# Scores of the second layer from 32 rows of the matrix array, issued in batches of four

## What is computed

```python
for layer in (0, 1):
    h = layernorm(x) * (1 + ca) + sa
    x = x + ga * attention(h)
    h = layernorm(x) * (1 + cb) + sb
    x = x + gb * experts(h)          # 8 experts; top 1 in layer 0, top 2 in layer 1

# attention of layer 0: causal
dots = q @ k.T * scale ; masked ; softmax ; @ v ; @ Wout.T + bout
# attention of layer 1: not causal, and followed by a second attention over two past states
output = softmax(q @ k.T * scale) @ v @ Wo + bo
rq = output @ Wrq + brq ; rk, rv = past @ Wrk + brk, past @ Wrv + brv     # 2 x 256 past tokens
rctx = mean over the two pasts of softmax(rq @ rk.T * scale) @ rv
gate = sigmoid([output, rctx] @ Wg + bg)
output = output * (1 - gate) + rctx * gate
```

## Time and profile before

| | |
|---|---|
| median of 3 runs | 1052.02 us |
| time of the profiled execution | 1054.27 us |
| span of its trace | 1052.3 us |
| PE busy | 960.2 us, 91% |
| DVE busy | 788.7 us, 75% |
| ACT busy | 591.6 us, 56% |
| POOL busy | 228.7 us, 22% |
| scores of layer 1 | from 360.71 us to about 894 us |
| experts of layer 1 and the end | from about 895 us |

### The profile page before, as it was taken

One profiled execution on the slowest core, in us unless ns is written; L12 is line 12 of the kernel. 1 busy time (PEld: TensorE's weight loads), 2 busy tenths in 40 slices (PEclk: granted clock), 3 DMA queues, 4 the chain that ended last, 5 costly groups with the idle time before them and its releaser, 6 DMA issues.

```text
span 1052.3 us, 17558 instructions
## 1 busy us (share of the span) xinstructions
PE 960.2 (91%) x5970; PEld 639.5 (61%) x5970; DVE 788.7 (75%) x2196; ACT 591.6 (56%) x1270; POOL 228.7 (22%) x360
## 2 busy tenths in 40 slices
PE   8889998888878989999999999999899887999992
PEld 7555665555668645555555555555555442999992
DVE  6888888776465698778888788978878784686673
ACT  2466565454555445767677676775567656443330
POOL 6132323263213234000000100001032112120073
PEclk8899999898989989999999999999999989999996
DMA  4334310010112111110000000000070000212132
GB/s 124 91 99 138 91 51 21 11 50 12 36 37 75 29 28 31 31 41 2 1 11 21 11 1 2 21 14 8 1 260 21 1 3 29 74 44 61 34 86 68
DMA packets 56497, 46.50 MB, mean 44 GB/s; under 512 B 6742, under 2 KB 46038, under 8 KB 56408
## 3 DMA queue, kind: packets, MB, share of 16 engines
q1 hardware_dynamic: 41960, 33.77, 11.4%
q0 software_dynamic: 3072, 6.30, 2.1%
q10 hardware_dynamic: 11376, 5.32, 1.8%
HBM read 22.55 MB, written 14.16 MB: 35 GB/s over the span
## 4 chain that ended last, share of the span: by engine, by line
PE 66%; DVE 20%; POOL 5%; issue 4%; ACT 2%; DMA 2%; DVEq 1%; SPq 0%; POOLq 0%; ACTq 0%
PE st L1346 13%; PE pv L1368 13%; PE ring L1332 12%; PE ring L1249 7%; PE ring L1469 4%; DVE ring L1653 4%; PE st L1456 3%; PE ring L1260 2%; PE ring L1299 2%; DVE M L1649 2%; PE st L1462 2%; DVE M L1656 2%; PE pv L1462 2%; POOL G L1041 1%; PE pv L1279 1%
## 5 line engine op out<-in xcount | busy, mean ns | idle before, releaser
L1123 ACT ACTIVATE Et<-st 128x512 f32<-128x512 f32 (+3 forms) x768 | 380.9, 548 | 211.9 <-PE st L1346 208.2
L1332 PE MATMUL ring<-Kbd,Qa 128*128 128x512 f32 (+3 forms) x512 | 203.3, 417 | 17.4 <-DVE M L1653 7.7
L1346 PE MATMUL st<-Qb,Kbd 128*128 128x512 f32 (+3 forms) x512 | 196.4, 399 | 4.4 <-ACT Et L1123 4.3
L1656 DVE TENSOR_REDUCE M<-ring 128x1 f32<-128x512 f32 x256 | 163.8, 683 | 38.4 <-PE ring L1332 37.0
L1649 DVE TENSOR_REDUCE M<-ring 128x2 f32<-128x512 f32 x256 | 162.9, 683 | 28.6 <-PE ring L1332 27.8
L1346 PEld LDWEIGHTS st<-Qb,Kbd 128*128 128x128 f32 x512 | 96.9, 195 | 89.6 <-ACT Et L1123 65.5
L1332 PEld LDWEIGHTS ring<-Kbd,Qa 128*128 128x128 f32 x512 | 100.6, 200 | 61.8 <-DVE M L1656 19.7
L1653 DVE CUSTOM_DVE_ANT_0 ring<-ring,maskw 128x128 f32<-128x128 f32 (+3 forms) x256 | 120.7, 510 | 20.9 <-PE ring L1332 19.5
L1368 PE MATMUL pv<-Et,Va 128*32 128x512 f32 (+3 forms) x1024 | 120.9, 533 | 0.7 <-POOL Et L984 0.7
L1332 PE MATMUL ring<-RKbd,Qa 128*128 128x512 f32 x256 | 108.2, 430 | 7.0 <-DVE M L1649 6.3
L1346 PE MATMUL st<-Qb,RKbd 128*128 128x512 f32 x256 | 105.4, 427 | 1.2 <-ACT Et L1123 1.0
(11 more groups left out here) (222 smaller groups left out, 1263.6 us busy)
## 6 DMA issues: line engine op xcount, KB each, us to landing
Kbd<-Ksb SPq DMA_DIRECT2D x116, 64.0 KB, 2.0
Yd<-Yt ACTq DMA_DIRECT2D x76, 64.0 KB, 1.5
Xs<-Xd SPq DMA_DIRECT2D x16, 256.0 KB, 3.0
L1W<-in_L1W SPq DMA_DIRECT2D x2, 2048.0 KB, 11.8
Xd<-zero SPq DMA_DIRECT2D x6, 512.0 KB, 3.5
W<-in_L0W SPq DMA_DIRECT2D x8, 258.0 KB, 3.5
W<-in_L0W SPq DMA_DIRECT2D x8, 256.0 KB, 4.2
Xd<-zero SPq DMA_DIRECT2D x4, 448.0 KB, 4.4
```

The lines of the kernel that those rows point to most:

```text
L1123: e.activation(Et[s // 2 % 4][:, j % 2, q0:512], st[s % NST][:, q0:512], ACT.Exp, scale=SCALE).then_inc(exp_done, 1)
L1332: ins = nc.tensor.matmul(bank(ph)[:, 0:n], Qa[u % 2][:, t * 128:(t + 1) * 128], kb[:, j, 0:n], start=True, stop=True)
L1346: nc.tensor.matmul(st[s % NST][:, q0:512], kb[:, j, c * 128:(c + 1) * 128], Qb[u % 2][:, q0:512], start=True, stop=True).then_inc(st_full, 1)
L1656: e.tensor_reduce(M[i][:, t, j, 0:1], bank(ph)[:, 0:n], AX.X, ALU.max).then_inc(mx_red, 1)
```

## The change

Layer 0 is left as it is. In layer 1:

- `mx` and `st` of head j multiply 32 rows instead of 128: `Qa[32j:32j+32]` by the keys on the same partitions, which are now simply the transposed keys (`KT` for self units, `RKT` for the past). ScalarE writes these straight from PSUM. The DMAs from `Ksb`, the block diagonals, their zeroing by GpSimd and the semaphores for them are gone in layer 1.
- The order of the plan is new. `mx` and `st` come in pairs every second step: heads 2 and 3 of the one beside heads 0 and 1 of the other, then the other way round. So four matmuls in a row stand on four different strips of 32 rows and write to four different banks. `pv`, `kT`, `qT`, `qbT`, `norm` and the other generators are started on the odd steps between. `FRONT`, `BACK` and others get a value for each layer.
- `ones_ahead`: one or two products of ones are put ahead of `rq`, `oTr` and `gate`, ahead of each pair of `mx` in units 0 and 1 of layer 1, and ahead of each pair of `st` in units 29 to 31. They go into the bank that the phase will overwrite.
- The end of the second attention (`epi_rec`: `oTr`, `gate`, `blend`) starts 9 or 5 steps later for the first two sequences and 3 for the third, and `token_rows` of layer 1 start 1 and 7 steps later. The wait in `mcol` to `qbT` is 3 steps instead of 4.

```diff
-KPREP, QPREP, FRONT, BACK = 2, 7, 10, 34
-AFTER_MAX, FINISH, PREP = 4, 2, -24
+KPREP, QPREP, FRONT, BACK = (2, 3), 7, (10, 12), (34, 36)
+AFTER_MAX, FINISH, PREP = (4, 3), (2, 3), (-24, -23)
...
+def ones_ahead(ph):
+
+    if ph[0] in ("rq", "oTr", "gate"):
+        return 2
+    if ph[0] == "mx" and ph[1] == 1 and ph[2] < 2 and ph[4] % 2 == 0:
+        return 2
+    return 1 if ph[0] == "st" and ph[1] == 1 and ph[2] >= 29 and ph[4] % 2 == 0 else 0
...
     def front(l, u, unit):
         for t in range(4):
...
+            else:
+                for j in (2, 3):
+                    do("mx", l, u, t, j)
+                yield from wait(2)
+                for j in (0, 1):
+                    do("mx", l, u, t, j)
+                yield from wait(2)
...
     def back(l, u, unit, starts, at):
...
+            do("st", l, u, c, 0)
+            do("st", l, u, c, 1)
+            yield
+            if c:
+                do("pv", l, u, c - 1)
+            yield
+            do("st", l, u, c, 2)
+            do("st", l, u, c, 3)
+            yield from wait(2)
+        yield from wait((3, 1)[l])
         do("pv", l, u, 3)
...
     def leftovers():
 
-        for j in range(4):
-            do("zKbd", j)
-        yield
         do("zQK")
+        yield
...
-        for g in range(4):
-            for j in range(4):
-                yield from wait(2)
-                do("zRK", g, j)
...
-            prep.append((64 * k + 116, epi_rec(b, k)))
-    prep += [(330, token_rows(1, 0)), (386, in_turn(token_rows(1, 1), route(1, 0))), (424, layer1_weights()),
+            prep.append((64 * k + (125 if b == 0 else 121), epi_rec(b, k)))
+    prep += [(331, token_rows(1, 0)), (393, in_turn(token_rows(1, 1), route(1, 0))), (424, layer1_weights()),
...
-                                 (490, in_turn(epi_rec(2, 6), token_rows(1, 2), route(1, 1))), (16 * 31 + BACK + 21, experts(1)),
...
+                                 (493, in_turn(epi_rec(2, 6), token_rows(1, 2), route(1, 1))), (16 * 31 + BACK[1] + 21, experts(1)),
...
-        RKbd = at("RKbd", [128, 4, 4, 512], F32R, fw0)
+        RKT = at("RKT", [128, 4, 512], F32R, fw0)
...
+        KT = [at(f"KT{i}", [128, 512], F32R, kbd0 + 2048 * i) for i in range(3)]
...
-                elif what == "kT" and a not in DIRECT:
-                    l, u = a
+                elif what == "kT" and a[0] == 0 and a[1]:
+                    u = a[1]
...
-                elif what == "pastK":
-                    g, = a
-                    sp.wait_ge(*taken(ph))
-                    sp.wait_ge(z_rk, 4 * (g + 1))
-                    for j in range(4):
-                        r = slice(32 * j, 32 * j + 32)
-                        e.dma_start(RKbd[r, g, j, :].bitcast(F32), Ksb[g % 2][r, :].bitcast(F32)).then_inc(rkbd_in[g % 2], 16)
...
+                    else:
+                        act.wait_ge(*keys_let_go(u))
+                        evict(ph, KT[u % 3][:, :])
                 elif what == "pastK":
                     g, = a
-                    gone = ksb_let_go(ph)
-                    act.wait_ge(gone[0], gone[1])
-                    evict(ph, Ksb[g % 2][:, :])
+                    experts_over()
+                    evict(ph, RKT[:, g, :])
...
+            def ones(bank):
+
+                if ones_ahead(ph):
+                    pe.wait_ge(z_ones, 1)
+                for _ in range(ones_ahead(ph)):
+                    nc.tensor.matmul(bank[:, 0:128], onesM[:, :], onesM[:, :], start=True, stop=True)
...
+                    r = slice(32 * j, 32 * j + 32) if l else slice(0, 128)
...
+                    nc.tensor.matmul(bank(ph)[:, 0:n], Qa[u % 2][r, t * 128:(t + 1) * 128], keys[:, 0:n],
+                                     start=True, stop=True).then_inc(mx_full, 1)
...
+                    keys = RKT[r, g, :] if kind == "rec" else KT[u % 3][r, :] if l else Kbd[u % 3][:, j, :]
...
+                    ones(st[s % NST])
                     pe.wait_ge(*taken(("qbT", l, u)))
-                    nc.tensor.matmul(st[s % NST][:, q0:512], kb[:, j, c * 128:(c + 1) * 128], Qb[u % 2][:, q0:512],
+                    nc.tensor.matmul(st[s % NST][:, q0:512], keys[:, c * 128:(c + 1) * 128], Qb[u % 2][r, q0:512],
                                      start=True, stop=True).then_inc(st_full, 1)
```

More of the change, by code:

```diff
@@ L158, in front @@
         for t in range(4):
-            for j in range(4):
-                do("mx", l, u, t, j)
-                yield
+            if l == 0:
+                for j in range(4):
+                    do("mx", l, u, t, j)
[5 more added lines that the diff above has]
+                for j in (0, 1):
+                    do("mx", l, u, t, j)
+                yield from wait(2)
         do("mcol", l, u)
-        yield from wait(AFTER_MAX)
+        yield from wait(AFTER_MAX[l])
         do("qbT", l, u)
@@ L167, in normal @@
     def normal(l, u):
-        yield from wait(FINISH)
+        yield from wait(FINISH[l] if (l, u) != (1, 31) else 0)
         do("norm", l, u)
@@ L172, in back @@
         for c in range(4):
-            for j in range(4):
[L174 to L180, removed]
+            if l == 0:
+                for j in range(4):
+                    do("st", l, u, c, j)
+                    yield
+                    if c and j == 2:
+                        do("pv", l, u, c - 1)
+                continue
+            do("st", l, u, c, 0)
+            do("st", l, u, c, 1)
+            yield
+            if c:
+                do("pv", l, u, c - 1)
+            yield
+            do("st", l, u, c, 2)
+            do("st", l, u, c, 3)
+            yield from wait(2)
+        yield from wait((3, 1)[l])
         do("pv", l, u, 3)
@@ L411, in plan @@
     do("kT", 0, 0)
-    pipeline(0, L0_UNITS, [(64 * b + PREP, prep_qkv(0, b, b)) for b in range(1, NB)]
+    pipeline(0, L0_UNITS, [(64 * b + PREP[0], prep_qkv(0, b, b)) for b in range(1, NB)]
              + [(64 * b + 106, epi0(b)) for b in range(2)]
@@ L691, in program, with kbd_ready, keys_let_go, last_max @@
         n_add = {ph: n for n, ph in enumerate(p for p in order if p[0] == "norm" and units[p[1]][p[2]][0] == "rec")}
[L692 to L696, removed]
+        kbd_no = [sum(v % 3 == u % 3 for v in range(1, u)) for u in range(16)]
+        L1_KEYS = [u for u, unit in enumerate(L1_UNITS) if unit[0] != "rec"]
         def earlier(ph, names, same):
             return next((p for p in order[:spot_of[ph]][::-1] if p[0] in names and same(p)), None)
[L702 to L709, removed]
+        def kbd_ready(u):
+            return kbd_in[u % 3], 64 * (kbd_no[u] + 1)
+        def keys_let_go(u):
+            had = [v for v in L1_KEYS if v < u and v % 3 == u % 3]
+            return st_full, n_st[("st", 1, had[-1], 3, 3) if had else ("st", 0, 15, 3, 3)] + 1
+        def last_max(l, u):
+            return n_mx["mx", l, u, 3, (3, 1)[l]] + 1
         def filled(ph):
@@ L1267, in _ @@
                     take(ph)
+                    ones(bank(ph))
                 if what == "modcol":
@@ L1339, in _ @@
                     q0 = 128 * c if l == 0 else 0
-                    kb = RKbd[:, g] if kind == "rec" else Kbd[u % 3]
+                    r = slice(32 * j, 32 * j + 32) if l else slice(0, 128)
+                    keys = RKT[r, g, :] if kind == "rec" else KT[u % 3][r, :] if l else Kbd[u % 3][:, j, :]
                     if s >= NST:
@@ L1769, in _ @@
                     elif l == 1:
-                        for m, v in kbd_unit[-2:]:
-                            dve.wait_ge(kbd_in[v % 3], 64 * (kbd_no[m, v] + 1))
-                        for i in range(2):
-                            dve.wait_ge(rkbd_in[i], 128)
+                        for u in (14, 15):
+                            dve.wait_ge(*kbd_ready(u))
                     e.memset(r["sums"][:, :, 0:4], 0.0)
```

96 lines of the change are left out of this document (40 added, 56 removed).

## The result

The changed kernel takes 1039.72 us (median of 4 runs, 1035.45 to 1042.85), the kernel before 1052.34 beside it: ratio 0.9879, interval 0.9836 to 0.9923. So 12.6 us are gained where 48 were forecast. The span is 1039.0 us. The page of the kernel after: its busy times (before: the earlier trace rows) and the granted clock in 40 slices of 26 us.

The account below looks back on a forecast made before the run. TensorE was taken to set the pace from 392.40 to 818.06 us; gains of 33 + 12 + 3 + 1.5 − 2 = 47.5 from 1054.3 gave 1006.8, and the median 2.25 lower, 1004 us; range 978 to 1044 us.

Parts of the forecast that it names:

- The batch: Layer 1 scores: four matmuls on different strips take 0.40 us together (0.25 to 0.56), against 0.23 each one by one.
- that rival: Layer 1 score batches: weights load in line, 0.56 us a batch, 37 us gained, 1015 us; chance 0.15.
- the one without overlap: Layer 1 score batches: strips don't overlap, 0.93 us a batch, kernel 1090 us; chance 0.04.
- the held-back rival: Layer 1 batches: a late maximum or exponential stops four matmuls, kernel 1032 us; chance 0.10.
- the forecast's 3.0 us less a unit: Layer 1 units: TensorE falls by 7.42 − 3.2 − 1.2 = 3.0 us, from batching less new changes of shape.
- VectorE sets the pace at 92%: 392.40 to 701.80 us: VectorE takes over, 92% full; the stretch takes 276 us, 33 gained.
- From 701.80 us on: 701.80 to 818.06 us: 12 us gained (9 to 18); to 876.17 us, with expert routing: 3 (0 to 7).
- the clock rival: Layer 1: the clock falls to half, 11.3 us more for each such unit, kernel 1074 us; chance 0.08.
- 0.95 was the mark: Layer 1: a granted clock under 0.95 would show the forecast wrong.
- Products of ones: Layer 1, ahead of `mx`, `rq`, `oTr`, `gate` and `st`: 0.23 us each, together 2 us lost (0 to 8).
- The order: Layer 1: `token_rows` delays of 1 to 7 steps cost nothing; later `gate` takes some 2.5 us off a projection unit.
- The start: 360.71 to 392.40 us: one copy replaces four to `Kbd`, 1.5 us gained (0 to 2.4).

Follow-up runs that it names:

- the shorter maxima: Changed kernel without layer 1's products of ones, maxima over half of the keys and exponential scaled by 1/8: 999.57 us, ratio 0.9346.
- the idles gone: Changed kernel without layer 1's products of ones, blend gap, later token rows, fewer VectorE instructions for `rq`: 1012.25 us (32 rows), 1009.84 us (64).
- The delays with 32 rows: Changed kernel without layer 1's products of ones; VectorE repeats one maximum 4, 6 and 8 times in units 3, 6 and 10: ratio 0.9934.
- the order alone: Kernel before, scores still on 128 rows, in the new order of the plan without products of ones: 1063.67 us, ratio 1.0114.
- the run with rows alone: Kernel before with layer 1's scores on 32 rows, in the old order, without products of ones: 1107.97 us, ratio 1.0544.
- shared strips: Changed kernel without layer 1's products of ones, each `mx` pair on the same two strips as the `st` pair beside it: 1111.86 us, ratio 1.0415.

## Why the prediction was right and wrong

- *The batch* (0.40 us taken, 0.25 to 0.56, and 0.15 for the change of shape): right where nothing holds it, 0.43 with the change of shape. The loads of four strips don't stand in line, so that rival falls, and so does the one without overlap. Part of the held-back rival came true, in batches of 0.67 to 0.76 us and over. With the shorter maxima, where TensorE is the bound again, the light unit takes 10.94 us, and the forecast's 3.0 us less a unit give 13.97 − 3.0 = 10.97.
- *VectorE sets the pace at 92%*: right in the light units, 12.04 us with VectorE at 11.11. Units 1 to 20 were to take 276 us: 282.70 in the changed kernel, 277.31 without products of ones, 276.01 with the idles gone. That these end at 276 is in part luck: VectorE's busy time, taken as unchanged at 250.59 us, was 242.60, and it was 86% to 88% full over the stretch. The unit with projections took 19.27 us (18.14 without products), not 16 to 17.
- *From 701.80 us on* (12 and 3 gained): wrong. Units 21 to 30 took 9.3 us more than before, 24 off. The clock stood at 0.87 and 0.65 here. The eight units from 21 on came down from 133.85 us to 131.09 without products, and with the idles taken away to 122.52 (32 rows) and 120.87 (64).
- *The clock* was the step that failed: the sum has no term for it. The forecast kept, layer 0 at 1.00 with TensorE 92% busy, as its reason, gave the clock rival 0.08, and said itself that no row tests 32 rows. Its sign came true: 0.89 where 0.95 was the mark, low for 90 us more than before. What was missed is, first, that with fewer rows the clock falls after shorter idles and mostly stays low longer (0.98, 0.90 and 0.81 in the old order, where TensorE hardly stands), and second, that making VectorE the bound makes TensorE idle, in lumps of 1 to 3 us where VectorE's order has something long ahead of the maxima.
- *What the 36 missing us are made of* isn't settled. The rival's price of 11.3 us in each 24.8 spent low gives 41 us for the 90, more than is missing, though the order and the products, below, cost time too. The delays with 32 rows give 9 us for 33 spent low, so some 25 for 90, an estimate. With 11 for the order and 8 beyond the price of the products that is 44: the parts overlap, or one is too high.
- *Products of ones* (2 lost, 0 to 8): mis-sized, 10 to 17 lost. The traces of the 31 units show 486.24 us with and 471.69 without; units 0, 1, 13, 21, 29 and 30 make up 12.9 of these 14.6. That they raise the clock at the start isn't borne out: 0.70 with and 0.66 without in unit 0.
- *The order* (its delays go without effect, and `gate` later saves 2.5): wrong, 11 us lost with 128 rows. Unit 14, of 14.62 us, takes 18.22 with the order alone.
- *The start* (1.5 gained): 3 lost in the changed kernel, 0.35 gained without the products (392.05 for 392.40).

The Trainium skill, TensorE: Matmul & The Clock Gate, section Part 1: The HAM clock gate, says that the gate follows how busy the array has been. The falls after idles agree; the ten microseconds at 0.51 with TensorE busy 10.00 of 10.00 us speak against busy time alone as the measure.

What stays open is why fewer rows keep the clock low, and why products of 128 rows put between them don't raise it. That the clocks of the two orders fall with the rows is shown; that each fall lasts longer with fewer rows rests on nine delays of unequal length, one profile for each size, and only six of the nine bear it out.

## What to carry to other kernels

When an edit hands the bound from TensorE to another engine, look for the places where that engine's order has a long step or a wait ahead of what TensorE needs, and take these idles away with the same edit. Price a microsecond at the low clock as its own term, and if the product uses only part of the rows, expect falls to come sooner and to last longer; here half of the rows two at a time was worth as much as a quarter four at a time. Don't fill gaps with idle products unless a run shows that they hold the clock.

## What the hardware showed that was not expected

- Four matmuls of 32 rows and 512 columns on four strips, two into each of two sets of banks, take 0.43 us from the start to the next phase where nothing holds them; four of 64 rows, two at a time, take 0.66 us, yet make the light unit only 0.25 us longer (12.30 against 12.05).
- In the run with rows alone TensorE was busy 20.96 of 22.40 us at a clock of 0.55; with shared strips low lasted from 592 to 650 us without a break.
- Eight instructions of VectorE over 128 columns make the high and low parts of `rq`; two over 512 take 0.67 us less of VectorE (12.49 us for 13.16 in unit 13).
